# Context, energy and projection products of a cross-attention and spline-FFN kernel: plain float32 matmuls or three f32r products of high and low parts

## The reference, cut to what matters

```
query = ctx @ Wq.T + bq ; key = ctx @ Wk.T + bk      # 512 x 128 each
attention = softmax(query @ key.T)                   # energy, 512 x 512
x = x + layernorm(x) @ attention.T
gate_w, up_w, down_w = cubic splines through control points
x = x + (silu(layernorm(x) @ gate_w.T) * (layernorm(x) @ up_w.T)) @ down_w.T
```

## Time and profile before

| | |
|---|---|
| median of three runs | 312.27 us |
| the profiled execution | 310.22 us |
| its span (first to last instruction) | 308.4 us |
| PE busy | 279.8 us (91%) |
| DVE busy | 183.0 us (59%) |
| POOL busy | 162.5 us (53%) |
| ACT busy | 155.2 us (50%) |
| mean granted PE clock | 0.945 of full |

### The profile page before, as it was taken

The page is one execution under the profiler, slowest core; times in us unless marked ns, Lnnn a source line. Parts: engine busy times, 40 slices in busy tenths (PEclk is TensorE's granted clock), DMA queues, the critical chain, the costliest instruction groups (busy, mean ns, idle before and its releaser), DMA issues.

```text
span 308.4 us, 3946 instructions
## 1 busy us (share of the span) xinstructions
PE 279.8 (91%) x1232; PEld 200.8 (65%) x1232; DVE 183.0 (59%) x319; ACT 155.2 (50%) x261; POOL 162.5 (53%) x141
## 2 busy tenths in 40 slices
PE   0757499977999999999999999999999999899995
PEld 0322134756477788884777888947778889377894
DVE  0389885897645676663466766634667666443503
ACT  1424244223588891334888913348889133286710
POOL 4099546387656466214564662145646621398630
PEclk9998555895999999999999999999999999999999
DMA  7999436000070000011800000117000001100003
GB/s 203 254 402 384 180 92 251 0 0 0 0 307 36 2 1 2 0 68 68 339 1 0 0 0 0 68 68 272 0 0 0 0 0 68 70 0 1 2 0 136
DMA packets 6950, 25.25 MB, mean 82 GB/s; under 512 B 1308, under 2 KB 1820, under 8 KB 5084
## 3 DMA queue, kind: packets, MB, share of 16 engines
q1 hardware_dynamic: 6940, 25.13, 22.6%
HBM read 20.93 MB, written 4.19 MB: 81 GB/s over the span
## 4 chain that ended last, share of the span: by engine, by line
PE 77%; DVE 9%; DMA 5%; SPq 3%; ACT 2%; issue 2%; POOL 1%; DVEq 0%; ACTq 0%; POOLq 0%
PE bank L1242 10%; PE bank L1273 10%; PE bank L1244 10%; DMA coef<-in_g_coef 5%; PE bank L1259 5%; PE bank L1257 5%; PE bank L1256 5%; PE bank L1228 4%; PE bank L1180 4%; PE bank L1203 4%; PE bank L1202 4%; PE bank L1204 4%; PE bank L1119 3%; PE bank L1280 3%; PE bank L1161 3%; PE bank L1217 3%
## 5 line engine op out<-in xcount | busy, mean ns | idle before, releaser
L1076 POOL TENSOR_TENSOR il<-inter,ih 128x512 fp32r<-128x512 f32 x64 | 86.3, 1361 | 44.6 <-ACT ih L762 24.9
L928 DVE TENSOR_TENSOR inter<-inter,bank 128x512 f32<-128x512 f32 x64 | 43.7, 686 | 44.7 <-ACT inter L758 44.6
L758 ACT ACTIVATE inter<-bank 128x512 f32<-128x512 f32 x64 | 37.9, 596 | 16.2 <-PE bank L1244 13.6
L762 ACT ACTIVATE ih<-inter 128x512 fp32r<-128x512 f32 x64 | 39.3, 630 | 2.5 <-DVE inter L928 2.3
L733 ACT ACTIVATE qk<-bank,nmr,rstd 128x512 f32<-128x512 f32 x16 | 12.5, 780 | 43.4 <-PE bank L1204 26.0
L1273 PEld LDWEIGHTS bank<-d_r,ih 128*128 128x128 f32 x256 | 32.6, 191 | 1.8 <-ACT ih L762 0.7
L1273 PE MATMUL bank<-d_r,ih 128*128 128x256 f32 x256 | 33.4, 284 | 0.0
L1064 POOL TENSOR_TENSOR xres<-x,ones 128x2048 f32<-128x2048 f32 x4 | 14.4, 3600 | 27.7 <-DMA out<-xres 25.8
L1242 PE MATMUL bank<-xh,gate_r 128*128 128x512 f32 x64 | 27.0, 422 | 1.7 <-DVE zg L920 1.7
L1256 PE MATMUL bank<-ih,d_u 128*128 128x512 f32 x64 | 27.9, 436 | 0.0
L1202 PE MATMUL bank<-ph,xh 128*128 128x512 f32 x64 | 26.0, 407 | 0.0
(11 more groups left out here) (94 smaller groups left out, 524.5 us busy)
## 6 DMA issues: line engine op xcount, KB each, us to landing
x<-in_x SPq DMA_DIRECT2D x4, 1024.0 KB, 4.8
xT<-in_xT SPq DMA_DIRECT2D x4, 1024.0 KB, 6.9
out<-xres SPq DMA_DIRECT2D x16, 256.0 KB, 2.1
ctxT<-in_ctxT SPq DMA_DIRECT2D x4, 512.0 KB, 7.5
rd<-in_d_r SPq DMA_DIRECT2D x2, 1024.0 KB, 6.0
knots<-in_d_knot SPq DMA_DIRECT2D x1, 1280.0 KB, 13.8
d_pt<-in_d_node SPq DMA_DIRECT2D x1, 1024.0 KB, 19.7
d_coef<-in_d_coef SPq DMA_DIRECT2D x1, 1024.0 KB, 21.7
```

The costliest lines, as they stand in the source:

```text
L758: nc.scalar.activation(inter[:, m % 3], gbank[m % 2][:], ACT.Silu).then_inc(s["silu_done"], 1)
L762: nc.scalar.activation(ih[:, m], inter[:, m % 3], ACT.Copy).then_inc(s["ih_done"], 1)
L928: V.tensor_tensor(inter[:, m % 3], inter[:, m % 3], ubank[m % 2][:], ALU.mult).then_inc(s["mult_done"], 1)
L1076: G.tensor_tensor(il[:, m % 2], inter[:, m % 3], ih[:, m].bitcast(f32), ALU.subtract).then_inc(s["il_done"], 1)
```

## The change

It does five things.

1. `qk(a)` and `energy(a, t)` for batches 1 to 3 are three f32r products each time (high x high, low x high, high x low) instead of one plain float32 product; batch 0 keeps plain float32. `project` is done so for all four batches.
2. The parts are made by ACT (a copy that rounds) and DVE (a difference): for wqk and g_basis once, in the start; for the context once a round, in the new stage `split_ctx(a)` at the head of `ffn` (128 x 1024 elements on each engine), into the space of xl; for query and key by two new DVE instructions in `qk(a)`, into the space of zd. `cast_t` now rounds straight into xn2r on ACT, and DVE takes the low part xn2l from PSUM.
3. `qk(a)` moves to right behind `project(b)` in the list, so on ACT it now comes before the first silu (before, it came behind the fourth silu and third round). On PE it was already right behind `project`.
4. The two lists have a new order, and the loads too: wqk and ctxT come first, coef before knots, g_basis after the energies of batch 0, since it lies in the space of qk.
5. The context of batch b + 2 is loaded when `split_ctx` has read the one before.

```diff
 def project / qk / energy, on PE
-            pe.wait_ge(s["xn2t_copied"], NT * (b + 1))
+            pe.wait_ge(s["xn2r_done"], NT * (b + 1))
             pe.wait_ge(s["node_done"], 2 * CLS)
             for a in range(CLS):
-                last = mm(zgbank[0:G_K, :], g_basis[:, a], xn2T[:, a], start=a == 0, stop=a == CLS - 1)
+                pe.wait_ge(s["xn2l_done"], NT * b + a + 1)
+                mm(zgbank[0:G_K, :], g_basis_h[:, a], xn2r[:, a], start=a == 0, stop=False)
+                mm(zgbank[0:G_K, :], g_basis_l[:, a], xn2r[:, a], start=False, stop=False)
+                last = mm(zgbank[0:G_K, :], g_basis_h[:, a], xn2l[:, a], start=False, stop=a == CLS - 1)
...
+                pe.wait_ge(s["ctx_split"], b)
+                pe.wait_ge(s["wqk_split"], 1)
+                pe.wait_ge(s["xn2l_done"], NT * b)
...
-                    last = mm(abank[n][:], wqk[:, n, c], ctxT[:, c], start=c == 0, stop=c == CTX // P - 1)
+                        mm(abank[n][:], wqk_h[:, n, c], ctx_h[:, c], start=start, stop=False)
+                        mm(abank[n][:], wqk_l[:, n, c], ctx_h[:, c], start=False, stop=False)
+                        last = mm(abank[n][:], wqk_h[:, n, c], ctx_l[:, c], start=False, stop=stop)
...
+                mm(abank[t % 2][:], qk_h[:, 0, c], qk_h[:, 1], start=True, stop=False)
+                mm(abank[t % 2][:], qk_l[:, 0, c], qk_h[:, 1], start=False, stop=False)
+                last = mm(abank[t % 2][:], qk_h[:, 0, c], qk_l[:, 1], start=False, stop=True)
 def split_ctx, on ACT and DVE
+            act.wait_ge(s["ctx_in"], 16 * (b + 1))
+            act.wait_ge(s["xm_mm"], NT * b)
+            nc.scalar.activation(ctx_h, ctxT[:], ACT.Copy).then_inc(s["ctx_hi"], 1)
...
+            dve.wait_ge(s["ctx_hi"], b)
+            V.tensor_tensor(ctx_l, ctxT[:], ctx_h.bitcast(f32), ALU.subtract).then_inc(s["ctx_split"], 1)
 def qk, on DVE
+            V.scalar_tensor_tensor(qk_l[:, n], abank[n][:], bqk[:, n:n + 1], qk_h[:, n].bitcast(f32), ALU.add, ALU.subtract)
 def cast_t, on ACT and DVE
-            nc.scalar.activation(xn2T[:, t], abank[t % 2][:], ACT.Copy)
-            V.tensor_copy(xn2r[:, t], xn2T[:, t])
+            nc.scalar.activation(xn2r[:, t], abank[t % 2][:], ACT.Copy)
+            V.tensor_tensor(xn2l[:, t], abank[t % 2][:], xn2r[:, t].bitcast(f32), ALU.subtract)
```

More of the change, by code:

```diff
@@ L329, in xattn_spline_ffn_kernel, with first @@
         s = {n: sem(n) for n in names.split()}
+        def first(b):
+            return isinstance(b, int) and b == 0
         def attention_only(st):
             st.constants()
-            st.split_windows(0)
             st.powers(0)
-            for t in range(1, 3):
[L340 to L346, removed]
+            st.split_weights()
+            st.qk(0)
+            for t in range(2):
+                st.split_windows(t)
+            for t in range(2):
+                st.energy(0, t)
+            st.split_windows(2)
+            st.softmax(0, 0)
+            st.energy(0, 2)
+            for t in range(1, 3):
+                st.powers(t)
+            st.softmax(0, 1)
+            st.powers(3)
+            st.energy(0, 3)
@@ L347, in attention_only @@
             st.spread(0)
             for t in range(2, 4):
[L349 to L352, removed]
-                st.spread(r)
[L354 to L362, removed]
+                st.softmax(0, t)
@@ L382, in attention_only @@
[L382 to L394, removed]
+            st.split_x(0)
+            st.spread(7)
+            st.mean_shift(0)
@@ new lines, in attention_only @@
+            st.down_factors()
+            st.prob_t(0, 3)
+            st.node_weights(4)
+            st.split_prob(0, 2)
+            st.node_weights(5)
+            st.split_basis()
+            st.node_weights(6)
+            st.split_prob(0, 3)
+            st.node_weights(7)
+            st.xm(0, 0)
+            st.jumps()
+            st.xm(0, 1)
+            st.down_nodes()
+            st.residual(6)
+            st.xm(0, 2)
+            st.spread(8)
+            st.xm(0, 3)
+            st.spread(9)
@@ L408, in attention_only @@
-            st.xm(0, 3)
+            st.cast_t(0, 0)
+            for r in range(10, 12):
+                st.residual(r)
+            st.cast_t(0, 1)
+            for r in range(12, 14):
+                st.residual(r)
+            st.cast_t(0, 2)
             st.spread(12)
-            st.residual(12)
+            st.norm_t(0, 2)
+            st.residual(14)
             st.spread(13)
[L412 to L415, removed]
@@ L454, in ffn @@
+            st.down_basis(b, 1)
+            st.round_inter(b, 4)
+            if a is not None:
+                for t in range(2):
+                    st.energy(a, t)
+                st.softmax(a, 0)
+            st.round_inter(b, 5)
+            if a is not None:
+                st.softmax(a, 1)
             st.down_basis(b, 2)
             st.gate_up(b, 6)
+            if a is not None:
+                st.stats(a)
+            st.activate(b, 6)
+            st.gate_up(b, 7)
+            if a is not None:
+                st.energy(a, 2)
```

324 lines of the change are left out of this document (182 added, 142 removed).

## The result

The changed kernel takes 324.4 us (median of four runs, 320.9 to 326.0), the one before 311.75 beside it (four, 310.5 to 312.3): a ratio of 1.038, 95% interval 1.032 to 1.044. So it is slower, as forecast, but by 12.7 us instead of 3.7, and outside the range. The profiled execution took 324.81 us, its span is 323.0: 14.6 more than before.

What follows compares the result with a forecast made beforehand. PE was taken to bound the loop, the order to decide the start. Start +0.3, three rounds +4.5 and last batch -0.9 gave +3.9 on 310.22; in its neighbours' terms 316.0 us, range 306.0 to 319.5.

Steps and rivals of the forecast that it cites:

- The sign and the rounds: Whole kernel slower; each of three rounds of the loop +1.5 us, bounds -2.1 and +2.2, together +4.5.
- wait 1: Head of a round: PE's query and key wait for the context's split behind ACT's table load; stall 0.8 us.
- wait 2: First silu: bias copies before it delay its table load, so PE stalls at gate tile 2, about 1.4 us.
- wait 3: Exponentials: 21.5 us chain with four loads against PE's 18.5; PE stands 3.0, including wait 2, tile 8 and the transposition.
- one load at the head: Rival, chance 0.15: the set loaded on entering a round already holds silu; a round +0.2, whole about 0, 312.3 us.
- What PE saves: f32r products save PE 2.1 us a round, three rounds, and 0.9 in the last ffn; sum 7.2 us.
- The last batch's term: Last ffn: only the projection gets shorter, 3.68 to 2.76 us, all on the path: -0.9 us.
- PE keeps its queue full: Rival, chance 0.2: PE saves all and waits are absorbed if chain and split_ctx are in time; -6.9, 305.4 us.
- The start: Before the first gate product: that product at 84.3 us against 84.0, +0.3, bounds -3 and +3.
- I place the new list from the rows: Start: stage times taken from the profile; scaled probabilities at 21.6, nodes to 49, residual 7 to 60.7, gate at 84.3.
- The rivals for a late start: Rival, chance 0.1: residual 8 late for rd and a low clock at the first rounds; +3, 319.0 us.

Runs made afterwards that it cites:

- the last kernel: Changed kernel with two added POOL waits, ffn's old list, query and key in two parts, final transpositions set apart by down tails; 304.8 us, ratio 0.980 to before.
- POOL kept off: Changed kernel, but POOL begins the powers after three windows are split and its down_nodes products after DVE's d_u; 316.3 us, ratio 1.016 to before.
- the statistics later: Changed kernel with only DVE's batch statistics moved from before the seventh product by up to behind the thirteenth; 333.0 us.
- the second wait alone: Changed kernel with one added wait: POOL's products of d_coef start only after DVE's d_u; 316.7 us.

## Why the prediction was right or wrong

**The sign and the rounds were right.** By its own steps, forecast and found, in us a round: wait 1, 0.8 and 0.67; wait 2, 1.4 and 1.47; wait 3 at tile 8, 0.3 and 0.49; before the transposition, 1.3 and 1.18; six table loads, six. The load as the row had it (1.34 from load to exp; after, 102.41 to 103.70 is 1.29) decided it. The rival *one load at the head* is refuted: there is a load at the head and a second one before silu, with only copies between.

The term **"What PE saves"** was too large. A round's PE work is its length less its gaps, 61.92 - 0.47 before and 63.95 - 4.17 after, so 1.7 saved and not 2.1: a plain product is two steps of 0.43, so the products give back 1.9 (24 x 0.4285 less 36 x 0.233), and behind each wait the first f32r product takes 0.31 to 0.33 to the next. With it a round is -1.7 + 3.7 = +2.0 instead of +1.5, near the bound of 2.2. The last batch's term of 0.9 was too large by the same reading: the 3.68 of the earlier trace rows holds the tail of the last matmul. From the start of the projection to the gate product it was 5.15 (262.50 to 267.65) and is 4.49, so 0.66 saved. Rounds and last batch together: +5.6 for +3.6.

*PE keeps its queue full* failed at the point it named: context's difference and the chain were both late. It could be had, though: in the last kernel the old order of `ffn` hides the chain, and its 60.2 us are close to what this rival said (61.85 - 2.1 = 59.8).

**The start was wrong**, +9.0 for +0.3, and this makes the miss. The step that failed is "I place the new list from the rows": every duration was taken from where the instruction stood before, and moved as if it depended on itself alone. (Its PE sum of 26 us is 27 by its own terms; that is not what failed.) The scaled probabilities came at 27.0 and not 21.6; nodes, at half clock as placed, ended at 57.3 and not 49, since nmr and d_u held the second half of them up (5.19 us idle before 53.56); DVE's part of residual 7 ended at 69.5 and not 60.7. The rivals for a late start, rd landing late and a low clock for query and key, weren't it: residual 8 started on the heels of its transfer (76.89, issued at 69.54), and query and key stepped at 0.23. With POOL kept off, every later milestone is where it was placed: residual 7 at 60.7, residual 8 at 68.1, the gate at 84.28 for 84.3. In part by luck: the probabilities were then still 2.2 late (23.8), and this was given back behind them, by the reckoning above 1.0 to 1.4 of it by the four node products at full clock, of which I had made a bound; the rest I can't place.

The mechanism is in the rows: a DVE operation with two inputs from SBUF that starts beside a running POOL one takes longer, whatever its size, by 0.1 to 0.2 us less than what was left of POOL's: xl in a round 0.27 with 0.40 left, xl in the start 0.53 with 0.66 left, the split at 15.11 of before 0.73 with 0.92 left, nmr 1.06 and each lengthened d_u 1.07 with 1.20 left. It looks like waiting for POOL's instruction to end. POOL's get longer too (d_coef 4.94 to 7.42, one of the four 3.31 beside xl). The Trainium skill says why in "SBUF — State Buffer", section Who interferes with whom: DVE and GpSimd have one pair of ports in common, which is a lock held for a whole instruction; a DVE instruction with two inputs from SBUF contends with a GpSimd one that reads SBUF. The rows agree: win_hl, nmr, d_u and xl have two such inputs and wait, while gate_v and prod, with a bank as one input, keep 0.74 and 0.68. With one input from SBUF both happen: the scaling of probabilities above took 1.49 for 0.48 and a cast of before, at 78.31, 1.49 for 0.42, while the statistics (bst, 0.67 to 0.70) and the reciprocal (0.18) keep their length beside POOL everywhere. The prediction didn't weigh this rule, though the row at 15.11 of before (1.47 for 0.75) shows it.

## What to carry to other kernels

When an instruction is moved, ask what runs beside it in its new place. For DVE operations with two inputs from SBUF, casts and scalings look at POOL's timeline there, and if the two can be put one behind the other with a wait, the wait may be worth many times its length. And take the parts of a change apart: the products here were worth nothing in the old order, cost 12.7 us in the new one, and gained 2% once the waits they bring and POOL's collisions were cleared.

## What the runs showed of the hardware

- The penalty beside POOL is no share of DVE's instruction but what is left of POOL's: nmr on 128 x 4 goes from 0.16 to 1.22, a window split on 128 x 512 from 0.74 to 1.74, xl on 128 x 2048 from 2.28 to 2.81. It is 1.0 to 1.1 at most here, which fits POOL's instructions in these rows, 1.27 us by themselves; no row shows such a DVE operation held up by a longer one. Small ones are hit hardest for their size.
- PE's clock in the node products doesn't follow the wait ahead of the last energies. After 5.17 us idle, in the changed kernel, all eight products ran at half clock; after 4.93 us, with the statistics later, the first four ran at full clock, as they did after 2.06 us with POOL kept off. PE timelines, the changed kernel and the one with the statistics later:

```profile
19.75 3.78 PE L1200 MATMUL bank<-qk 128*128 128x512 f32 x4 [5.17 <-ACT prob L691]
...
31.59 2.03 PE L1266 MATMUL bank<-power,coef 64*102 64x512 f32 x2
```

```profile
20.24 3.78 PE L1200 MATMUL bank<-qk 128*128 128x512 f32 x4 [4.93 <-ACT prob L691]
...
32.08 1.19 PE L1266 MATMUL bank<-power,coef 64*102 64x512 f32 x2
```

- The same kernel can have the collision in one run and hardly in the next: three splits took 5.19 us in the changed kernel's profile and 3.08 in that of the kernel with the second wait alone, whose windows and powers are the same.
